# A gated cross-attention block: the four heads interleaved, the warming products and the second input moved, and a new order for the fill

## The chip, the cores and the metric

One core of a Trainium2 chip (trn2). The metric is the device time of one execution in microseconds (us). The kernel is written engine by engine: TensorE (PE: matrix products and transposes), VectorE (DVE), ScalarE (ACT), GpSimd (POOL), and SyncE (SP), which issues most DMAs. Each engine works through its own list in order; semaphores tie the lists together.

## What is computed

```python
x = x + tanh(g_xattn[0]) * xattn(layernorm(x), ctx, mask, rms_scale, q_w, kv_w, out_w)
x = x + tanh(g_ffn[0])   * ffn(layernorm(x), W1, b1, W2, b2)

def xattn(x, mem, mask, rms_scale, q_w, kv_w, out_w):        # 4 heads, 1 key/value head, 64 wide
    xn, mn = rmsnorm(x, rms_scale), rmsnorm(mem, rms_scale)
    q = rope(einsum('BTD,NDH->BTNH', xn, q_w), S + t) / 8
    k, v = einsum('BSD,cKDH->cBSKH', mn, kv_w);  k = rope(k, s)
    p = softmax(where(mask, q k^T, -2.4e38));    return einsum('BTNH,NHD->BTD', p v, out_w)

def ffn(x, W1, b1, W2, b2):                                   # weights made ternary: -1, 0 or 1
    return gelu(x @ ternary(W1).T + b1) @ ternary(W2).T + b2
```

x is 4 x 1024 x 256, the context 4 x 154 x 256, the FFN 1024 wide; all float32.

## The kernel before

The 4096 rows of x are eight groups of 512 (four tiles of 128 rows), two groups to each of the four batches. A group goes through: transposing x (`x_T`), projecting it to q (`project`, `q`), the rotation (`rotate` on DVE with `rope`, `add_rotated` on POOL), transposing q (`q_T`), the scores of two heads at a time (`scores`), mask and row minimum (`mask_and_min`), exponentials (`exps`), division (`normalise` on POOL), transposing the probabilities (`p_T`, `tail_T`), the product with values that have Wo already in them (`attend`), residual, second normalisation, and the FFN (`ffn_in`, gelu, `ffn_out`). To keep float32 accuracy in the quick fp32r format, every operand is split into a rounded part ("hi", on ACT) and a remainder ("lo", on DVE), and products are made of two or three such pairs. FFN work of a group is done in the step after its attention.

The order of the work is written out by hand for each engine: a function `fill` for what comes before the loop, which is the preparation of the weights and groups 0 (`FIRST`) and 1 (`SECOND`) woven together (`BEFORE` is the group ahead of the first), and a function `step` that runs for groups 2 to 9, the last two of which only finish. Semaphores count in that order. The lists `FILL_T`, `FILL_M` and `FILL_H` name the order in which the pairs of PSUM banks `ps_t`, `ps_m` and `ps_h` are used, and so which use waits for which.

What the fill prepares:
- `keep_warm` makes products of ones that nobody reads. `spread_pairs` and `spread_rows` put the RMS scales onto partitions, by products with a single row; `gate_row` holds the two gate values and comes by a DMA of its own.
- The context (`ctx_sb`) is transposed (`context_T`), scaled while it is copied (`copy_context`), and multiplied by Wk (`k_products`) and by Wv side by side twice (`v_products`). Its norms come from `context_sums` and `context_norms` on DVE and a power on POOL.
- `rotate_k` and `add_rotated_keys` rotate the keys, `k_T` transposes them, `kk_rounded` and `kk_rest` split them into `kk_hi` and `kk_lo`. Two heads share a score product: their queries stand in partitions 0 to 63 and 64 to 127, and the keys stand once in the upper half of the partitions and once in the lower half of a second set of columns, the rest zero (two memsets of POOL).
- Wq is scaled by ACT (`scale_wq`), its column sums are made by TensorE (`sum_wq`), DVE takes off their 256th part (`centre_wq`), and ACT and DVE split it (`wq_rounded`, `wq_rest`). This takes the layernorm's mean out of x.
- `vw_product(n)`, twelve of them, multiply values by Wo; `vw_rounded` and `vw_rest` split them. `VW_ON_POOL` could name some for POOL; it is empty. `w_low_piece` on POOL and `ternary` on DVE make the FFN weights ternary, in eight pieces.

SP's DMAs in order: the context, its four tails, x of group 0, the key tables, the q tables, Wo twice, W1, W2, x of group 1, b1. ACT's: the identity, the RMS scales, the gates, Wk, Wv, Wq.

## Time and profile before

| | |
|---|---|
| median of three runs | 308.92 us (308.06 to 309.13) |
| the profiled execution | 309.19 us; its span, first to last instruction, 307.4 us |
| TensorE busy | 295.4 us (96%), 2119 products and transposes |
| DVE busy | 243.2 us (79%) |
| ACT busy | 234.3 us (76%) |
| POOL busy | 131.1 us (43%) |
| DMA | 13.27 MB, most of what the weights and tables need in the first 20 us |

The page's slices (one digit a fortieth of the span, tenths of it busy):

```
PE   5996999989999999999999999999999999999996
DVE  2589899999987889779886899878977897567443
ACT  2596787898697967897588959796788958883581
```

Times in rows count from the span's start. A row of the timeline gives start, duration, engine, line, operation, what is written and what is read ("ps_t<-ident_sb,q_cos": the moving operand first, then the one loaded as weights) and the shape. Matmuls and DVE instructions are pipelined: the next one starts before the last one's printed end, so a rate is read from starts. A float32 product shows as two instructions, an fp32r product and a transpose as one.

### The profile page before, as it was taken

How to read it: one execution, taken by the hardware profiler on the slowest of the kernel's cores; microseconds unless marked ns; L12 is line 12 of the kernel's file. 1: busy time of each engine (PE TensorE's matmuls, PEld its weight loads, DVE VectorE, ACT ScalarE, POOL GpSimd, SP SyncE). 2: the span in 40 equal slices, each digit the busy share in tenths (PEclk: the TensorE clock that was granted, in tenths of full speed). 3: DMA queues.
4: the chain of work that ended last, by engine and by line, in shares of the span. 5: the costliest groups of instructions: out<-in, count | busy, mean ns of one | idle time of the engine just before them, and what ended most of it. 6: DMA issues, size and time to landing. Idle time of an engine off the chain costs nothing.

```text
span 307.4 us, 6780 instructions
## 1 busy us (share of the span) xinstructions
PE 295.4 (96%) x2119; PEld 274.6 (89%) x2119; DVE 243.2 (79%) x819; ACT 234.3 (76%) x601; POOL 131.1 (43%) x152
## 2 busy tenths in 40 slices
PE   5996999989999999999999999999999999999996
PEld 5975999878999899989998899989998999889886
DVE  2589899999987889779886899878977897567443
ACT  2596787898697967897588959796788958883581
POOL 8376878692246305522334414630542333511300
PEclk9999899999999999999999999999999999999999
DMA  6970000200202002100201010100210000100202
GB/s 204 286 243 2 0 3 0 71 0 2 69 3 68 2 0 70 53 17 2 68 13 55 0 54 15 51 17 0 71 52 17 2 0 11 61 3 0 70 0 68
DMA packets 12281, 13.27 MB, mean 43 GB/s; under 512 B 823, under 2 KB 11696, under 8 KB 12256
## 3 DMA queue, kind: packets, MB, share of 16 engines
q1 hardware_dynamic: 11452, 12.29, 12.6%
q10 hardware_dynamic: 708, 0.46, 0.5%
q0 software_dynamic: 96, 0.21, 0.4%
q8 instruction: 13, 0.21, 0.3%
q14 instruction: 12, 0.10, 0.1%
HBM read 8.76 MB, written 4.19 MB: 42 GB/s over the span
## 4 chain that ended last, share of the span: by engine, by line
PE 85%; DVE 7%; issue 2%; ACT 2%; DMA 1%; POOL 0%; ACTq 0%; DVEq 0%
PE ps_m L1293 22%; PE ps_h L1293 22%; PE ps_m L1526 17%; PE ps_s L1293 9%; PE ps_t L1301 4%; PE ps_t L1471 4%; PE ps_t L1447 2%; DMA gate_row<-in_gates 1%; PE ps_t L1546 1%; PE ps_m L1546 1%; DVE s_neg L1025 1%; PE ps_t L1479 1%; DVE pT_lo L938 1%; ACT hT_hi L699 1%; ACT h_all L699 1%
## 5 line engine op out<-in xcount | busy, mean ns | idle before, releaser
L487 POOL TENSOR_TENSOR prob<-prob,p_inv 128x512 f32<-128x512 f32 x32 | 34.2, 1069 | 66.8 <-DVE p_inv L1041 66.7
L1086 DVE TENSOR_TENSOR hT_lo<-h_all,hT_hi 128x512 fp32r<-128x512 f32 x64 | 42.2, 686 | 18.6 <-ACT hT_hi L699 18.6
L1293 PE MATMUL ps_h<-x1nT_hi,w_tern 128*128 128x512 f32 x128 | 54.4, 425 | 1.2 <-ACT hT_hi L699 0.9
L1526 PE MATMUL ps_m<-w_tern,hT_hi 128*128 128x256 f32 x224 | 55.2, 287 | 0.0
L1526 PE MATMUL ps_m<-w_tern,hT_lo 128*128 128x256 f32 x224 | 53.6, 279 | 0.0
L665 ACT ACTIVATE prob<-s_neg,s_min 128x154 f32<-128x154 f32 x128 | 52.4, 416 | 1.2 <-DVE s_min L1036 1.1
L699 ACT ACTIVATE h_all<-ps_h,b_sb 128x512 f32<-128x512 f32 x64 | 44.6, 697 | 8.2 <-PE ps_h L1293 7.0
L1293 PE MATMUL ps_h<-x1nT_lo,w_tern 128*128 128x512 f32 x128 | 50.6, 395 | 0.0
L463 POOL TENSOR_TENSOR q_cos<-q_cos,q_sin 128x256 f32<-128x256 f32 x32 | 23.6, 738 | 58.4 <-DVE q_sin L992 57.6
L1293 PE MATMUL ps_m<-vw_hi,pT_hi 128*128 128x256 f32 (+1 forms) x160 | 45.5, 284 | 0.0
L1293 PE MATMUL ps_m<-vw_hi,pT_lo 128*128 128x256 f32 (+1 forms) x160 | 44.8, 280 | 0.0
L1293 PE MATMUL ps_m<-vw_lo,pT_hi 128*128 128x256 f32 (+1 forms) x160 | 44.7, 279 | 0.0
L699 ACT ACTIVATE hT_hi<-ps_h,b_sb 128x512 fp32r<-128x512 f32 x64 | 44.7, 698 | 0.0
L1526 PEld LDWEIGHTS ps_m<-w_tern,hT_lo 128*128 128x128 f32 x224 | 42.2, 188 | 0.0
L1526 PEld LDWEIGHTS ps_m<-w_tern,hT_hi 128*128 128x128 f32 x224 | 42.1, 188 | 0.0
L938 DVE TENSOR_TENSOR pT_lo<-ps_t,pT_hi 128x512 fp32r<-128x512 f32 (+1 forms) x64 | 30.2, 482 | 10.8 <-ACT pT_hi L642 10.7
L642 ACT ACTIVATE pT_hi<-ps_t 128x512 fp32r<-128x512 f32 (+1 forms) x64 | 27.3, 444 | 9.0 <-PE ps_t L1471 8.8
L1293 PEld LDWEIGHTS ps_m<-vw_hi,pT_hi 128*128 128x128 f32 x160 | 30.0, 188 | 1.2
L1293 PEld LDWEIGHTS ps_h<-x1nT_hi,w_tern 128*128 128x128 f32 x128 | 24.1, 188 | 7.4 <-ACT hT_hi L699 3.8
L1293 PEld LDWEIGHTS ps_m<-vw_lo,pT_hi 128*128 128x128 f32 x160 | 30.1, 188 | 0.6
L1293 PEld LDWEIGHTS ps_m<-vw_hi,pT_lo 128*128 128x128 f32 x160 | 30.0, 187 | 0.0
L642 ACT ACTIVATE qT_hi<-ps_t 128x256 fp32r<-128x256 f32 x32 | 12.1, 377 | 23.2 <-PE ps_t L1447 23.2
(162 smaller groups left out, 778.2 us busy)
## 6 DMA issues: line engine op xcount, KB each, us to landing
x_sb<-in_x SPq DMA_DIRECT2D x8, 512.0 KB, 3.5
out_x<-x_both SPq DMA_DIRECT2D x8, 384.0 KB, 2.5
h_all<-in_w1t SPq DMA_DIRECT2D x1, 1024.0 KB, 11.1
w_raw<-in_w2t SPq DMA_DIRECT2D x1, 1024.0 KB, 13.4
out_x<-x_both SPq DMA_DIRECT2D x8, 128.0 KB, 1.7
x_both<-in_ctx_main SPq DMA_DIRECT2D x1, 512.0 KB
wo_raw<-in_wo SPq DMA_DIRECT2D x2, 256.0 KB, 8.4
x_both<-in_wq ACTq DMA_DIRECT2D x1, 256.0 KB, 6.5
```

The source lines that it names most:

```text
L463: pool.tensor_tensor(q, q, swapped, ALU.add).then_inc(q_roped, 1)
L487: pool.tensor_tensor(main, main, inv.to_broadcast([P, H, P]), ALU.mult)
L642: nc.scalar.activation(dst, src, ACT.Copy).then_inc(t_hi, 1)
L665: e = nc.scalar.activation(prob[t][:, h, :], s_neg[t % 2][:, h, :], ACT.Exp, bias=s_min[t % 2][:, h:h + 1], scale=-1.0, accum_out=p_sum[:, ...
L699: g = nc.scalar.activation(dst, ps_h[c % 2][:], ACT.Gelu, bias=b1_sb[:, c:c + 1])
L938: dve.tensor_tensor(dst, src, hi, ALU.subtract).then_inc(t_lo, 1)
L1086: dve.tensor_tensor(hT_lo[:, c, :], h_act[c % 4][:], hT_hi[:, c, :], ALU.subtract).then_inc(h_split, 1)
L1293: m = pe.matmul(dst, lhs, rhs, start=(n == 0), stop=(n == len(pairs) - 1))
L1301: m = pe.transpose(dst[:, P * t:P * (t + 1)], src[:, t, P * k:P * (k + 1)], ident_sb[:])
L1447: m = pe.transpose(t_bank(s.i, f"q{t}")[:, P * a:P * (a + 1)], q_cos[t % 2][:, P * a:P * (a + 1)], ident_sb[:])
L1471: m = pe.transpose(t_bank(s.i, f"p{t}")[:, P * h:P * (h + 1)], prob[t][:, h, 0:P], ident_sb[:])
L1526: m = pe.matmul(dst, a[:, c, P * t:P * (t + 1)], w[:, c, :], start=(c == 0 and a is hT_hi), stop=(c == NF - 1 and a is hT_lo))
```

## The change

It has five parts. `SPLIT_ON_POOL` and the waits it brings in are empty: they yield the same waits as before.

1. *Interleaved heads.* Wq's columns are ordered so that a channel's four heads stand side by side (column = channel x 4 + head). The rotation reads the projection once and writes both products with one instruction of 128x512 on DVE, with a joined table `rq`, made on POOL in the fill by two copies. POOL's addition works on halves of 128 columns. `q_T` loads every other column of q. The keys stand doubled in neighbouring columns, and a parity column (1 or 0 for each partition) scales them into `kk_hi` and `kk_lo`, over all 128 partitions, so the two memsets go.
2. *Centring by a product.* A matrix (identity minus 1/256, scaled by row) is multiplied by Wq on TensorE; ACT and DVE split the result out of PSUM. `scale_wq`, `sum_wq` and DVE's `centre_wq` go.
3. *Warming.* `keep_warm` multiplies ones by 512 columns of zeros: four times before `spread_pairs`, once after. The later six products of ones go. `k_products` takes Wk and Wv side by side (128 columns; the second half is not used).
4. *DMAs.* The RMS scales go first on ACT's queue, two of the context tails move to it, the gates go last and have a product of their own (`spread_gates`). The second input is fetched before the q tables; group 0's transposed x lies in `x1nT_hi` and `x1nT_lo`, so group 1's need not wait for its use.
5. *Another order of the fill* on TensorE, ACT, DVE and POOL, and of the banks. All twelve value remainders are on DVE, as before. The order of `step` is the same.

```diff
@@ SP: DMAs
-            for b in range(B):
+            for b in range(2):
                 sp.dma_start(ctx_sb[TP * b:TP * b + TAIL, B, :], ctx_tail[b]).then_inc(ctx_in, 16)
...
+            sp.dma_start(x_sb[1][:], x_g[1]).then_inc(x_in[1], 16)
+            sp.dma_start(rq_cos, rope_q_cos).then_inc(rope_in, 16)
+            sp.dma_start(rq_sin, rope_q_sin.rearrange("p t j c -> p t (j c)")).then_inc(rope_in, 16)
...
-            sp.dma_start(x_sb[1][:], x_g[1]).then_inc(x_in[1], 16)
@@ POOL
-            pool.memset(kk_hi[:].bitcast(F32), 0.0).then_inc(zeros_set, 1)
-            pool.memset(kk_lo[:].bitcast(F32), 0.0).then_inc(zeros_set, 1)
+            pool.memset(centre_base[:, 0::2, :], -1.0 / D).then_inc(base_edges_set, 1)
...
+            def join_tables():
+                pool.wait_ge(rope_in, 32)
+                pool.tensor_copy(rq[:, :, 0].rearrange("p t (j c) -> p t j c", j=2),
+                                 rq_cos.rearrange("p t (o c) -> p t o c", o=1).to_broadcast(
+                                     [P, 2 * NT, 2, C // 2])).then_inc(rope_set, 1)
+                pool.tensor_copy(rq[:, :, 1], rq_sin).then_inc(rope_set, 1)
...
+                cos, sin = (q[t % 2].rearrange("p (j n) -> p j n", j=2) for q in (q_cos, q_sin))
+                pool.tensor_tensor(cos, cos, sin[:, ::-1, :], ALU.add).then_inc(q_roped, 1)
...
                 context_rstd()
                 scale_tables()
+                mask_biases()
+                rstd1(BEFORE)
+                join_tables()
                 add_rotated_keys()
@@ ACT
+            act.wait_ge(ctx_zeroed, 1)
+            for b in range(2, B):
+                act.dma_start(ctx_sb[TP * b:TP * b + TAIL, B, :], ctx_tail[b]).then_inc(ctx_in, 16)
...
+                for k in range(KD):
+                    nc.scalar.activation(centre[:, k].rearrange("p (a c) -> p a c", c=P), centre_base[:, 1 - k:3 - k, :],
+                                         ACT.Copy, scale=scale1[:, KD + k:KD + k + 1]).then_inc(centre_set, 1)
...
+                for j in range(2):
+                    for dst, src in kk_parts(kk_hi, S * j):
+                        nc.scalar.activation(dst, src, ACT.Copy, scale=parity[:, j:j + 1]).then_inc(kk_hi_set, 1)
@@ DVE
+                        dve.scalar_tensor_tensor(dst, src, parity[:, j:j + 1], hi, ALU.mult,
+                                                 ALU.subtract).then_inc(kk_set, 1)
...
-                dve.scalar_tensor_tensor(q_cos[t % 2][:].rearrange("p (a c) -> p a c", a=2 * H),
-                                         q.rearrange("p (a c) -> p a c", a=2 * H), r, cos, ALU.mult, ALU.mult)
...
-                dve.scalar_tensor_tensor(q_sin[t % 2][:].rearrange("p (h c) -> p h c", h=H),
-                                         q.rearrange("p (h c) -> p h c", h=H), r, sin,
+                tables = rq[:, pos].rearrange("p a (c o) -> p a c o", o=1).to_broadcast([P, 2, C, H])
+                twice = q.rearrange("p (o c h) -> p o c h", o=1, h=H).to_broadcast([P, 2, C, H])
+                dve.scalar_tensor_tensor(q_both[t % 2][:].rearrange("p a (c h) -> p a c h", h=H), twice, r, tables,
                                          ALU.mult, ALU.mult).then_inc(m_read, 1)
@@ DVE, the fill from wq_rest on (new order, to mask_and_min(FIRST, 0))
+                gate_norms()
+                sums1(FIRST)
                 wq_rest()
+                mask_of(FIRST)
                 v_rest(0)
+                v_rest(1)
                 rope_first(BEFORE)
+                sums1_there(FIRST)
+                variances1(FIRST)
+                rope(FIRST, 1)
+                kk_rest()
+                q_lo(FIRST, 0)
+                gate_tail_norms()
+                rope(FIRST, 2)
+                rope(FIRST, 3)
+                q_lo(FIRST, 1)
+                mask_and_min(FIRST, 0)
@@ TensorE
+            def keep_warm(n):
+
+                pe.wait_ge(zeros_set, 1)
+                zeros = prob_tail[:].rearrange("p t h s -> p (t h s)")
                 for _ in range(n):
-                    pe.matmul(dst[:, 0:P], ones_sb[:], ones_sb[:], start=True, stop=True)
+                    pe.matmul(ps_h[1][:], ones_sb[:], zeros, start=True, stop=True)
...
+            def centre_wq():
+                pe.wait_ge(centre_set, KD)
+                pe.wait_ge(wq_in, 16)
+                for k in range(KD):
+                    m = products(ps_m[0][:, H * C * k:H * C * (k + 1)],
+                                 [(centre[:, j, P * k:P * (k + 1)], wq_raw[:, j].rearrange("p (a g c) -> p c g a", a=HP, g=2)) for j in range(KD)])
+                m.then_inc(wq_centred, 1)
...
-                    m = pe.transpose(t_bank(s.i, f"q{t}")[:, P * a:P * (a + 1)], q_cos[t % 2][:, P * a:P * (a + 1)],
+                    m = pe.transpose(t_bank(s.i, f"q{t}")[:, P * a:P * (a + 1)],
+                                     q_cos[t % 2].rearrange("p (n a) -> p a n", a=HP)[:, a],
                                      ident_sb[:])
@@ TensorE, the fill's head
-                keep_warm(5)
+                keep_warm(4)
                 spread_pairs()
-                spread_rows()
+                keep_warm(1)
                 context_tail_T()
                 context_T(0)
                 context_T(1)
-                keep_warm(2)
+                spread_rows()
                 x_T(BEFORE, 0)
+                x_T(BEFORE, 1)
                 k_products()
-                x_T(BEFORE, 1)
-                sum_wq()
+                spread_gates()
+                centre_wq()
                 v_products(0)
-                keep_warm(4, ps_s[1])
+                tail_norms()
+                v_products(1)
                 k_T()
                 q_first(BEFORE)
```

## Rows read from the trace of the kernel before

**Rows 1.** By stage: start:end, length, each engine's busy us (instructions), clock, DMA, GB/s
```profile
12.50:20.00 7.50, 7.50 (x51) 6.44 (x51) 5.11 (x18) 4.46 (x10) 3.55 (x3) 1.00 1.05 331
20.00:28.30 8.30, 5.53 (x40) 4.61 (x39) 8.14 (x22) 6.38 (x12) 5.31 (x9) 1.00 0.09 27
28.30:56.40 28.10, 27.73 (x198) 26.34 (x198) 26.93 (x114) 22.66 (x83) 23.59 (x26) 0.94 0.01 1
56.40:79.50 23.10, 21.89 (x147) 19.12 (x147) 21.90 (x63) 20.22 (x42) 12.24 (x10) 1.00 0.07 24
79.50:280.60 201.10, 199.97 (x1475) 187.68 (x1474) 164.58 (x561) 161.89 (x424) 74.33 (x88) 1.00 0.09 30
```

**Rows 2.** Chain of waits, first 80 us: start, us, what
```profile
1.87 3.88 DMA gate_row<-in_gates
...
29.50 1.46 PE ps_s L1293 x6
```

**Rows 3.** DVE in order of time, 19.9 to 31.4 us: start, us, what
```profile
19.97 0.48 DVE L989 SCALAR_TENSOR_TENSOR q_cos<-ps_m,r,rq_cos 128x256 f32<-128x256 f32 x1 [0.32 <-PE ps_m L1293]
...
20.77 1.75 DVE L909 TENSOR_TENSOR kk_lo<-ps_s,kk_hi 64x512 fp32r<-64x512 f32 x4
...
24.46 1.39 DVE L952 BATCH_NORM_STATS2 bn<-x_sb 128x6 f32<-128x256 f32 x4
...
26.47 0.29 DVE L891 TENSOR_TENSOR hT_hi<-ps_h,hT_hi 64x128 fp32r<-64x128 f32 x1
...
28.33 0.30 DVE L1025 CUSTOM_DVE_ANT_0 s_neg<-ps_s,mask_now 128x154 f32<-128x154 f32 x1
...
30.69 0.74 DVE L916 SCALAR_TENSOR_TENSOR vw_lo<-ps_h,gate_r,vw_hi 128x512 fp32r<-128x512 f32 x1
31.35 0.31 DVE L1025 CUSTOM_DVE_ANT_0 s_neg<-ps_s,mask_now 128x154 f32<-128x154 f32 x1
```

**Rows 4.** TensorE in order of time, first 20 us (xN: merged instructions)
```profile
1.28 2.50 PE L1307 MATMUL ps_h<-ones_sb 128*128 128x128 f32 x10 [1.28 <-POOL ones_sb L378]
...
11.73 2.92 PE L1293 MATMUL ps_h<-x1n,prob 128*128 128x64 f32 x20
...
15.80 1.88 PE L1293 MATMUL ps_m<-prob 128*128 128x512 f32 x4
...
17.52 1.05 PE L1307 MATMUL ps_s<-ones_sb 128*128 128x128 f32 x8
```

**Rows 5.** POOL and TensorE's key transposes in order of time, to 20 us
```profile
1.16 0.53 POOL L379 MEMSET prob_tail<- 128x512 f32 x1
...
9.33 1.19 POOL L389 TENSOR_TENSOR ctx_r<-ctx_me,neghalf 128x5 f32<-128x5 f32 x1 [2.48 <-DVE ctx_me L860]
...
15.79 1.55 POOL L404 TENSOR_TENSOR x1n<-s_neg 128x640 f32<-128x640 f32 x1 [3.43 <-DVE s_neg L885]
...
18.41 0.71 PE L1374 MATMUL ps_s<-ident_sb,x1n 128*128 128x128 f32 x5
```

**Rows 6.** DMA issues, first 30 us: count, KB each, us to landing
```profile
h_all<-in_w1t SPq DMA_DIRECT2D x1, 1024.0 KB, 11.1
...
rq_sin<-in_rope_q_sin SPq DMA_DIRECT2D x1, 256.0 KB, 8.6
```

**Rows 7.** DVE by form: count, busy us, mean ns; idle before
```profile
L916 DVE SCALAR_TENSOR_TENSOR vw_lo<-ps_h,gate_r,vw_hi 128x512 fp32r<-128x512 f32 x8 | 6.0, 747 | 0.9 <-ACT vw_hi L631 0.9
...
L909 DVE TENSOR_TENSOR kk_lo<-ps_s,kk_hi 64x512 fp32r<-64x512 f32 x2 | 1.4, 684 | 0.0
```

**Rows 8.** TensorE's waits before the half-clock stretch, in order of time
```profile
23.48 0.39 PE L1293 MATMUL ps_m<-wq_hi,xT_hi 128*128 128x256 f32 x1 [0.93 <-DVE q_sin L992]
...
28.46 0.74 PE L1293 MATMUL ps_h<-hT_lo,hT_hi 128*128 128x512 f32 x2 [1.31 <-DVE gate_r_tail L902]
```

**Rows 9.** Transposes at half clock: the context's, strided, and x_sb's, unstrided
```profile
8.32 1.92 PE L1330 MATMUL ps_s<-ident_sb,x_both 128*128 128x128 f32 x8
...
10.88 1.06 PE L1301 MATMUL ps_t<-ident_sb,x_sb 128*128 128x128 f32 x4
```

443 lines of the change are left out of this document (221 added, 222 removed), and 8 rows, old and new, of the table FILL_T.

## The prediction, made before the changed kernel ran

> **What bounds the kernel now.** I read the busy time by stage first [rows 1]. The 307.4 us fall into three parts. From 79.5 to 280.6 us six groups of rows pass through the loop's order, and TensorE is busy 199.97 of 201.10 us: it bounds that part, while VectorE (DVE) has 36.5 us to spare. From 280.6 us there is the tail. Before 79.5 us lies the fill: preparing weights, keys and values, and groups 0 and 1. There DVE is busy 8.14 of 8.30 us, then 26.93 of 28.10, then 21.90 of 23.10. A queue so full works through its own list, so the fill's end is set by when DVE starts its dense list and by how long that list is. TensorE is close behind (27.73 of 28.10 us from 28.3 on, 3.4 us of it at the granted half clock, 1.2 GHz, visible as a mean of 0.94).
>
> The chain of waits says the same and shows the head [rows 2]: it runs through a DMA of two gate values (3.88 us), TensorE's small products and then DVE, until TensorE takes over at 29.50 with the second scores. So what the change does is worth something where it starts DVE's list earlier, shortens it, or changes TensorE's work in the loop.
>
> **The point to follow.** Group 0's first mask-and-minimum starts on DVE at 28.33 us [rows 3]. I place that point in the new order and carry the shift to the end.
>
> **Warming and head.** Before, five products of ones (ten instructions) take 2.50 us from 1.28, 0.21 us apart, and TensorE then waits for the gates. The same instruction stands 0.11 apart in the eight at 17.52 [rows 4]: half and full clock. (The granted-clock figure reads 1.00 there too; the spacing is what tells.) The clock rises inside the key products (11.73 to 14.65): twenty take 2.92 us, where all at half would take 4.3. By then TensorE had worked without a break for some 7 us, since the gates' DMA landed at 5.75 [rows 2]. Now four products of 512 columns (eight instructions) start once prob_tail is zero, at 1.7 us. A 512-column instruction takes 0.43 us at full clock (value product, 1.88 us for four) [rows 4], so twice that, 0.86, at half. All at half clock they end at 1.7 + 6.9 = 8.6 us; with the clock up after half of it, at about 7. I take 7.8, both ends kept. Then the pair scales are spread, and DVE, whose queue has the context sums behind them, starts these at 7.8 + 0.75 = 8.55 instead of 6.64 (0.75 us after the gates' wait ended at 5.89). What waits behind: the context norms, ready when POOL (GpSimd) started its power at 9.33 [rows 5], 2.7 us after the sums (now 11.2); on POOL that power of 1.19 us (12.4), the key tables, the mask bias and group 0's power, together 3.0 us (15.4; their order is new, their sizes are not). New on POOL, ahead of the key addition, are two copies of 512 values (join_tables). No row shows one: a memset of 512 values takes 0.53, the two-input addition of 640 takes 1.55, so 1.24 for 512 [rows 5]; I take 0.8, being one-input, so 1.6 us, 17.0. The key addition's 1.55 us makes 18.6, against 17.34 before. That hid under the value and warming products, since the key transposes started at 18.41 [rows 5]; now they start at 18.8: +0.4 us. If the warming ends at 8.6, it is +1.2; the price of the two copies moves it by −0.5 to +0.9. The memsets of kk_hi and kk_lo go, but POOL had been done with all memsets before its power at 9.33: nothing.
>
> **Queues.** SP issues two context tails fewer and the second input (512 KB) before the tables; about 0.9 us earlier and, at the 331 GB/s of that stretch [rows 1], 1.6 us of transfer later for all behind. The tables for q, last landing 8.6 us after issue at 4.91, 13.5, then land near 14.5, before POOL asks at 15.4; wo and the two FFN weights land 1 to 1.5 us later (w1 18.1 before, about 19.6 now) [rows 6], while ScalarE (ACT) sums them only behind the keys, after 20.7. ACT issues two tails before wk, wv and wq, 0.5 us net later; wq, landing near 9.5, is asked for at 13.9. All hidden, with about 1 us of cover for the tables.
>
> **Wq centring.** Gone: ACT's two scalings and DVE's two corrections of all of Wq, and four column-sum instructions of TensorE. New: the centring matrix is scaled by ACT (the same sizes) and multiplied by Wq, eight instructions of 256 columns. At half the 0.43 us of a 512-column one [rows 4] that is 1.72 us. In order: k products 11.5 to 13.75 (20 at 0.112, since a wider moving side of 128 columns still fits the 0.11 of the ones products), gates, centring to 15.7, value products 1.9+0.4 to 18.1. wq_lo is ready at about 17.4: hidden behind k_T. Its moving operand steps 512 bytes from value to value, which no row shows; I bound it by nothing and by what the same instruction takes at half clock, a doubling, +1.7 us, of which 1.1 would be late for the first projection. The first rope then starts at 20.2 (before 19.97).
>
> The Trainium skill (Advanced Engine Details and Errata, SBUF Cachelines) says that a line is 16 bytes, and that reading a new line for every value costs; by that the doubled price would hold. It also says two hits on a line suffice, which would leave the transposes below untouched; no row at full clock shows either.
>
> **DVE up to the point.** From the first rope to the point passed 28.33 − 19.97 = 8.36 us, nearly without idling [rows 3]. Leaving it: statistics of group 1 (from 24.46) and one x remainder, together 2.01 us to 26.47, then a value remainder and the mask, 0.5; the early second input allows the first, and these go into DVE's idle time before 20 us or behind the point. Each rope was two instructions, 0.79 us from 19.97 to 20.77; now it is one of 512 values from PSUM, like the value remainder of 0.66 us (30.69 to 31.35): −0.13 each, four of them −0.5. Coming in: group 1's variance 0.49, and the key remainders as scaled subtractions (747 against 684 ns for 512 values [rows 7], two large and two small) +0.15. Sum: 8.36 − 2.5 − 0.5 + 0.65 = 6.0; 20.2 + 6.0 = 26.2, or 2.1 us earlier. TensorE's scores need the keys at 24.1 and take 1 us: in time. The first value product, which waited for DVE until 28.46 [rows 8], can start near 25.2.
>
> **From the point to the loop.** All twelve value remainders were already on DVE (VW_ON_POOL is empty on both sides): zero. The list gains x remainder 0.60, loses the variance 0.49 and five rope pairs' 0.65: −0.5 us. DVE idles only 2.4 us between 28.3 and 79.5, which an order could halve but not remove; I count nothing. TensorE at half clock cost 3.41 us × ½ = 1.7 us; it had stood still for 0.93 us and 1.31 us just before [rows 8]. (The mean of 0.94 over 28.10 us is 3.4 us at half.) In the new order it has less to wait for, but while DVE sets the pace only part counts: 0.5 of 0 to 1.7. Towards 79.5 the FFN's gelus on ACT follow and start when ffn_in does, which waits for x1n's remainders in DVE's list: they move with it. Sum: −2.1 −0.5 −0.5 = −3.1 us.
>
> **The loop and the tail.** The step orders are unchanged. Four ropes a step save DVE 0.5 us where it is not the bound; POOL's addition loses a dimension of its pattern and keeps its length: zero. The scores have the same 308 columns with other zero rows. One thing touches TensorE: q's transposes load q_cos with a step of two values. The context transposes before do the same; eight of them took 1.92 us, or 0.213 each, and the four unstrided x_sb ones at that clock took 0.213 as well [rows 9]. At full clock the unstrided stand 0.11 apart (five key transposes in 0.71 us [rows 5]). Bounds: zero, or 64 × 0.104 = 6.7 us if the strided load stays at 0.213. I take zero, the equality at half clock being the nearest row.
>
> **Sum.** The profiled run took 309.19 us: a span of 307.4 and 1.79 around it. 309.19 − 3.1 = 306.1. It is 0.27 above the median of the three runs, 308.92; against that the forecast is 305.8 us.
>
> **The rivals.**
> - *Deeper gain, 303.2.* The half-clock stretch vanishes wholly (another −1.2) and the new order removes the TensorE waits of 1.2 us from 56.4 to 79.5. For it: TensorE carries the chain from 29.5 to 45. Against: DVE is 96% busy there.
> - *Slow centring, 307.0.* The strided moving operand doubles its 1.73 us: −3.1 + 1.1 to 1.7, less the cover. It is the skill's rule above, as a mechanism of this kernel.
> - *Given back, 308 to 309.8.* The warming at half clock ends late (+0.8), the copies hold the keys (+0.5), and in the fill TensorE and ACT (20.22 of 23.10 us from 56.4 on) are near enough to full that DVE's shift is lost there.
> - *Slower, 312.5.* The strided weight loads of q's transposes. Each 0.104 us is paid by the bounding engine, 64 times; from 0.05 us each it undoes the gain. Against: the equal 0.213. This is the one that ends on the other side.
> - *It does not do what it says:* the wide products, of zeros, might not lift the clock; then the head runs at half clock to 12.7 as before, +0.8, inside the range.
>
> **Chances.** Forecast (304.3 to 307.3 or so) 0.53; slow centring 0.12; deeper 0.12; given back 0.12, mostly within the bound; strided loads 0.07; 0.04 for an order that blocks a queue somewhere I did not walk. Runs of this kernel differ by 0.3%, 0.9 us, which is what a measurement can tell from no change. Faster by more 0.76, same 0.12, slower 0.12. The range must leave out no more than 2 in 10: from 302.4 (below it half of the deeper cases) to 309.2 (the strided loads and the rest above).
>
> **What would show it.** The warming row of eight instructions ending between 7 and 8.6 us, later gaps of 0.11; copies of 0.5 to 1.1 us on POOL; centring spacing 0.216 or 0.43; the first mask-and-minimum near 26.2 us; rope rows of 0.75 us, 32 of them; a loop step still 33.5 us (201.1 over six); q's transposes 0.109 apart; and the start of group 2's loop step near 76.4 instead of 79.5. It is wrong if that start comes late although the point came early (then DVE was not the bound), or if the loop's length moves by more than 0.5 us.

## The result

The change made the kernel slower, by 0.9%: 311.37 us median of 5 runs (310.71 to 312.39) against 308.92 beside it, a ratio of 1.0093 (95% interval 1.0072 to 1.0115). I had forecast 305.8. The profiled execution of the changed kernel took 312.39 us, the longest of its five and 1.0 above their median; its span is 310.6 us against 307.4.

Three stretches say where the time went. I cut the span at the point (group 0's first mask-and-minimum on DVE) and at the end of the fill (start of group 1's fourth residual, the 79.5 us of the prediction):

| us | to the point | point to end of fill | end of fill to the end | span |
|---|---|---|---|---|
| before | 28.33 | 51.15 | 227.91 | 307.4 |
| forecast | 26.2 | 50.15 | 227.9 | 304.3 |
| after | 30.13 | 51.12 | 229.35 | 310.6 |

All three missed: the point by 3.9 us, the fill behind it by 1.0, the loop and the tail by 1.4.

The busy time by stage, cut as in [rows 1]:

```profile
12.50:20.00 7.50, 7.50 (x37) 5.03 (x36) 5.47 (x21) 2.92 (x8) 3.93 (x6) 1.00 1.05 273
20.00:30.10 10.10, 7.90 (x49) 6.18 (x49) 8.53 (x20) 8.87 (x15) 5.99 (x6) 1.00 0.24 77
30.10:56.40 26.30, 25.86 (x198) 24.33 (x197) 25.96 (x104) 22.53 (x81) 25.18 (x30) 1.00 0.01 2
56.40:81.30 24.90, 23.51 (x156) 20.13 (x154) 23.03 (x63) 21.25 (x44) 12.05 (x11) 1.00 0.07 23
81.30:283.60 202.30, 201.25 (x1476) 189.36 (x1475) 163.90 (x539) 163.14 (x424) 74.36 (x88) 1.00 0.09 29
```

The half-clock stretch is gone (0.94 in [rows 1], 1.00 here), as hoped; in one of the other four runs the mean clock of the whole run was 0.994, which is what one such stretch leaves. But the DMAs moved 273 GB/s between 12.5 and 20 us where they had moved 331, and were still at work behind 20 us. DVE stands idle for 1.6 of the 10.1 us before the point, where it had idled 0.2 of 8.3. And the six groups of the loop's order took 202.3 instead of 201.1 us although no instruction was added there.

TensorE, and below it ScalarE, POOL and DVE, in order of time up to the first ropes (start, us, what; in brackets the wait before it):

```profile
1.83 5.11 PE L1351 MATMUL ps_h<-prob_tail,ones_sb 128*128 128x512 f32 x8 [1.83 <-POOL prob_tail L396]
...
11.79 1.09 PE L1343 MATMUL ps_t<-ident_sb,x_sb 128*128 128x128 f32 x8 [1.48 <-DMA x_sb<-in_x]
...
15.35 3.76 PE L1335 MATMUL ps_m<-x_both,prob 128*128 128x256 f32 x8
18.94 1.90 PE L1335 MATMUL ps_m<-prob 128*128 128x512 f32 x4
...
21.60 0.66 PE L1427 MATMUL ps_s<-ident_sb,x1n 128*128 128x128 f32 x4
```

```profile
20.95 1.06 ACT L651 ACTIVATE hT_lo<-wo_raw 128x1024 fp32r<-128x1024 f32 x1 [1.20 <-DMA wo_raw<-in_wo]
21.92 0.58 ACT L639 ACTIVATE hT_hi<-ps_m 64x512 fp32r<-64x512 f32 x1
...
23.73 1.75 ACT L647 ACTIVATE kk_hi<-ps_s,parity 128x512 fp32r<-128x512 f32 x4
```

```profile
18.88 0.61 POOL L409 COPY rq<-q_both 128x512 f32<-128x512 f32 x1 [2.39 <-DMA q_both<-in_rope_q_sin]
19.44 0.60 POOL L412 COPY rq<-q_both 128x512 f32<-128x512 f32 x1
20.01 1.54 POOL L427 TENSOR_TENSOR x1n<-s_neg 128x640 f32<-128x640 f32 x1
```

```profile
23.14 0.69 DVE L933 TENSOR_TENSOR hT_hi<-ps_m,hT_hi 64x512 fp32r<-64x512 f32 x1 [1.50 <-ACT hT_hi L640]
...
24.08 0.75 DVE L1032 SCALAR_TENSOR_TENSOR q_both<-ps_m,r,rq 128x512 f32<-128x512 f32 x1
```

Three chains end within half a microsecond of each other, each late. The value products end at 21.5. TensorE had stood 1.48 us waiting for group 0's own input, which is issued ahead of the early second one and 0.8 us sooner than before, and yet landed at 11.8 instead of 10.3 us; and the eight centring products took 3.76 us, 0.45 apart. These started at 15.35, right behind the products ahead of them: wq had landed at 15.0 and was not waited for. The key addition ends at 21.55, behind two copies that waited for rq_sin until 18.88 and themselves took 0.6 each. And ScalarE waited for wo until 20.95, rounds it ahead of the values, and so gave DVE the values at 23.1; DVE forms their remainders ahead of the first rope. That rope came at 24.08, forecast 20.2. Whoever takes one chain away finds the next. The DMA issues show why they are late, against [rows 6] (last column: us from issue to landing):

```profile
h_all<-in_w1t SPq DMA_DIRECT2D x1, 1024.0 KB, 14.1
...
wo_raw<-in_wo SPq DMA_DIRECT2D x2, 256.0 KB, 10.7
x_both<-in_wq ACTq DMA_DIRECT2D x1, 256.0 KB, 11.4
q_both<-in_rope_q_sin SPq DMA_DIRECT2D x1, 256.0 KB, 14.2
```

Wo and Wq in the kernel before:

```profile
wo_raw<-in_wo SPq DMA_DIRECT2D x2, 256.0 KB, 8.4
x_both<-in_wq ACTq DMA_DIRECT2D x1, 256.0 KB, 6.5
```

### The profile page after: what moved, and what is told of

It reads as the page before. It is cut to its first block, busy times and chain, and to the rows that moved or that the text cites. A ratio compares the mean times of both kernels' runs of the same rounds, so it can differ in the third digit from the quotient of the medians.

```text
span 310.6 us, 6748 instructions
## 1 busy us (share of the span) xinstructions
PE 299.0 (96%) x2111; PEld 272.4 (88%) x2111; DVE 243.3 (78%) x787; ACT 235.6 (76%) x601; POOL 130.6 (42%) x153
## 3 DMA queue, kind: packets, MB, share of 16 engines
q1 hardware_dynamic: 11374, 12.23, 12.5%
## 4 chain that ended last, share of the span: by engine, by line
PE 76%; DVE 9%; DMA 4%; ACT 3%; issue 3%; SPq 2%; POOL 2%; DVEq 0%; ACTq 0%
PE ps_m L1335 20%; PE ps_h L1335 20%; PE ps_m L1580 17%; PE ps_s L1335 7%; DMA wo_raw<-in_wo 4%; PE ps_t L1343 4%; PE ps_t L1525 4%; PE ps_t L1500 2%; DVE s_neg L1064 1%; DVE vw_lo L958 1%; PE ps_t L1600 1%; PE ps_m L1600 1%; DVE pT_lo L980 1%; PE ps_t L1533 1%; DVE q_both L1032 1%
## 5 line engine op out<-in xcount | busy, mean ns | idle before, releaser
L1580 PE MATMUL ps_m<-w_tern,hT_hi 128*128 128x256 f32 x224 | 56.2, 289 | 0.0
L1580 PE MATMUL ps_m<-w_tern,hT_lo 128*128 128x256 f32 x224 | 54.7, 282 | 0.0
L486 POOL TENSOR_TENSOR q_both<-q_both 128x256 f32<-128x256 f32 x32 | 24.2, 760 | 58.9 <-DVE q_both L1032 58.7
L675 ACT ACTIVATE qT_hi<-ps_t 128x256 fp32r<-128x256 f32 x32 | 12.2, 382 | 23.1 <-PE ps_t L1500 22.3
## 6 DMA issues: line engine op xcount, KB each, us to landing
x_both<-in_wq ACTq DMA_DIRECT2D x1, 256.0 KB, 11.4
```

The source lines that it names most:

```text
L486: pool.tensor_tensor(cos, cos, sin[:, ::-1, :], ALU.add).then_inc(q_roped, 1)
L675: nc.scalar.activation(dst, src, ACT.Copy).then_inc(t_hi, 1)
L1580: m = pe.matmul(dst, a[:, c, P * t:P * (t + 1)], w[:, c, :], start=(c == 0 and a is hT_hi), stop=(c == NF - 1 and a is hT_lo))
```

## The experiments

The table has each run's profile cut at the same two places, the median of all its runs and the ratio to the kernel before. Landings of the first DMAs differ from execution to execution, so "to the point" of a single profile is uncertain by about 1 us (28.33, 27.27 and 27.26 in before, e7 and e14, whose engines have the same work there); the other two repeat within 0.5 us where code and tiles are the same, and the last stretch lies between 227.88 and 227.93 in all four profiles of the old layout. Differences of a few tenths are read from it, not from medians.

| run | to the point | fill behind it | to the end | median us | ratio (95%) |
|---|---|---|---|---|---|
| e1_x1_behind_tables | 31.04 | 51.13 | 229.09 | 311.26 | 1.0078 (1.0056 to 1.0101) |
| e2_wq_contiguous | 28.45 | 50.74 | 229.13 | 310.73 | 1.0078 (1.0049 to 1.0106) |
| e3_both | 29.77 | 51.11 | 228.89 | 311.52 | 1.0060 (1.0022 to 1.0098) |
| e4_fill_order | 30.61 | 51.76 | 229.30 | 311.96 | 1.0096 (1.0066 to 1.0125) |
| e5_v_before_wo | 30.16 | 51.02 | 229.22 | 311.88 | 1.0085 (1.0056 to 1.0113) |
| e6_after_padded | 29.25 | 51.19 | 228.81 | 310.52 | 1.0054 (1.0030 to 1.0077) |
| e7_before_shifted | 27.27 | 50.79 | 228.90 | 309.86 | 1.0073 (1.0025 to 1.0121) |
| e8_three | 26.80 | 51.03 | 228.73 | 309.43 | 1.0019 (0.9989 to 1.0049) |
| e9_q_halves | 28.27 | 51.00 | 228.37 | 310.40 | 1.0057 (1.0029 to 1.0084) |
| e10_keys_first | 27.48 | 51.06 | 228.77 | 309.38 | 1.0024 (1.0001 to 1.0046) |
| e11_before_x1_early | 31.67 | 51.16 | 227.91 | 310.09 | 1.0048 (1.0012 to 1.0083) |
| e12_tails_on_sp | 26.95 | 51.03 | 228.75 | 309.19 | 1.0012 (0.9991 to 1.0033) |
| e14_before_tails_on_act | 27.26 | 51.03 | 227.93 | 308.93 | 1.0020 (0.9985 to 1.0055) |
| e15_pad_992 | 28.36 | 50.99 | 228.16 | 308.91 | 1.0011 (0.9985 to 1.0037) |
| e16_before_wide | 26.91 | 49.97 | 227.88 | 307.32 | 0.9956 (0.9924 to 0.9988) |
| e17_all_x1_late | 27.24 | 52.46 | 228.17 | 311.66 | 1.0086 (1.0057 to 1.0115) |
| e18_fill_and_fixes | 27.05 | 51.43 | 228.24 | 308.81 | 1.0016 (1.0000 to 1.0033) |

**Two suspects for the head, alone and together.** e1 moves the second input behind the query tables and its sums behind the mask copy:

```diff
-            sp.dma_start(x_sb[1][:], x_g[1]).then_inc(x_in[1], 16)
             sp.dma_start(rq_cos, rope_q_cos).then_inc(rope_in, 16)
             sp.dma_start(rq_sin, rope_q_sin.rearrange("p t j c -> p t (j c)")).then_inc(rope_in, 16)
+            sp.dma_start(x_sb[1][:], x_g[1]).then_inc(x_in[1], 16)
```

> The changed kernel (311.4 us) with one part undone: the second input is loaded behind the two query tables and ahead of wo, and its sums stand behind the mask copy on DVE. Theory A (the early second input delays what the head needs: rq_sin landed at 18.88 us and held POOL's joining copies, the key addition and so k_T at 21.6): rq_sin lands 3 us earlier, near 16, the key addition ends near 18.6, and k_T is then held by the value products (20.84 in the trace of after): 0.8 us earlier, 310.6 us. If wq lands earlier too (it landed at 15.0), the value products come forward with it and 2 to 2.5 us are gained, 309.2. Theory B (the strided centring alone holds the head): k_T is set by the PE's centring and value products either way, at most 0.3 us, 311.1.

Neither theory's time came. The key addition ended at 19.74 us, 1.8 earlier, and k_T still started only at 23.29, behind the products:

```profile
13.76 3.30 PE L1335 MATMUL ps_h<-x1n,prob 128*128 128x128 f32 x20
...
17.30 3.76 PE L1335 MATMUL ps_m<-x_both,prob 128*128 128x256 f32 x8
...
23.29 0.71 PE L1427 MATMUL ps_s<-ident_sb,x1n 128*128 128x128 f32 x5
```

The profiled run, 313.05, is not typical of its median: TensorE fell to half clock there from about 12.3 to 15.7 us (the twenty key products took 3.30 us, 2.40 in after, and the transposes ahead of them 1.87 instead of 1.09). Without these 1.7 us the products would have let k_T start near 21.6, as in after. So the tables alone were not what held it: the two chains ended together.

e2 orders wq's columns on the host:

```diff
-                                 [(centre[:, j, P * k:P * (k + 1)], wq_raw[:, j].rearrange("p (a g c) -> p c g a", a=HP, g=2)) for j in range(KD)])
+                                 [(centre[:, j, P * k:P * (k + 1)], wq_raw[:, j]) for j in range(KD)])
```

> The changed kernel with the columns of wq put in interleaved order on the host, so that the centring products read a contiguous moving operand; the same is computed. The eight centring products should be 0.22 us apart and no more 0.44, and take 1.8 instead of 3.8 us. Theory B (this is what the head lost): k_T and the first rope come 1.8 us earlier, 309.6 us. Theory A (k_T waits for the key addition behind the late tables, until 21.55 whatever the PE does): k_T does not move, 311.2 us, within 0.3 of the changed kernel.

The centring row of e2's profile:

```profile
15.03 1.99 PE L1335 MATMUL ps_m<-x_both,prob 128*128 128x256 f32 x8
```

So the strided moving operand had cost 1.8 us for eight instructions. In this profile rq_sin and wo landed earlier too, and the point came 1.7 us earlier; the median moved by 0.6. e3, both edits:

> Both edits of the two runs before together. If the two waits stand beside each other (key addition at 21.55, value products at 20.84), each alone hides behind the other and only both together bring k_T forward: to 18.8 to 19.3 us, 2.3 to 2.8 us earlier, 308.8 us, more than the sum of the two alone. If only one of them held the head, this equals that one.

k_T came at 19.07 us, as the joint theory said, and yet the first rope only at 23.72: 4.65 us behind it. That pointed at the third chain. TensorE, ScalarE and DVE:

```profile
19.07 0.71 PE L1427 MATMUL ps_s<-ident_sb,x1n 128*128 128x128 f32 x5
...
20.60 1.06 ACT L651 ACTIVATE hT_lo<-wo_raw 128x1024 fp32r<-128x1024 f32 x1 [3.12 <-DMA wo_raw<-in_wo]
...
23.72 0.75 DVE L1032 SCALAR_TENSOR_TENSOR q_both<-ps_m,r,rq 128x512 f32<-128x512 f32 x1
```

The medians of e2 and e3 carry something else besides. In both profiles TensorE fell to half clock between about 24 and 28 us, after it had stood still for 1.11 and 0.91 us (e2) and for 3.04 us (e3), waiting for DVE and POOL; thirteen of their fourteen runs have a mean clock of 0.988 to 0.994, against one of five of the changed kernel. What this took back of their gain is not separated here.

**The third chain: wo.** In all five profiles until then the first rope stood 3.1 to 3.4 us behind the rounding of wo. e5 moves that rounding behind the values on ScalarE:

```diff
-                wo_rounded()
                 v_rounded(0)
                 v_rounded(1)
+                wo_rounded()
                 kk_rounded()
```

> The changed kernel with one move in ScalarE's order: wo_rounded() stands behind the two v_rounded() instead of ahead of them. Theory W: the first rope waits for wo. In all five profiles of the changed kernel and its variants the first rope starts 3.1 to 3.4 us after wo_rounded (20.95 to 24.08, 21.59 to 24.99, 18.88 to 22.00, 20.61 to 23.72, 21.44 to 24.57), whatever k_T does, because ACT rounds wo ahead of the values and DVE forms v_rest ahead of the rope. Then the first rope comes at about 22.8 (values end at 21.5 in after), 1.2 us earlier, and starts no more at wo_rounded plus 3.1; time 310.3 us against 311.4. Rival (k_T, the key addition and the value products set it): first rope stays 2.5 us behind k_T, time 311.3.

```profile
22.81 1.06 ACT L651 ACTIVATE hT_lo<-wo_raw 128x1024 fp32r<-128x1024 f32 x1
...
23.16 0.75 DVE L1032 SCALAR_TENSOR_TENSOR q_both<-ps_m,r,rq 128x512 f32<-128x512 f32 x1
```

Theory W held for the rope, which came at 23.16, 1.7 us behind k_T and 0.35 behind the start of wo's rounding. It gained nothing: ScalarE's list was as long as before, with the keys' rounding still behind wo (22.81 + 1.06). DVE waited for it and then for q's rounding, 0.28 us each, and the point stayed at 30.16. Alone, the edit only changes which wait ends last.

**The loop.** Between the two kernels the products with w2 (ffn_out) had moved from 117 to about 120 ns apart, in every profile (the mean of 342 gaps in the loop is 117.2 ns in before and 119.4 in after). Their code is the same. What differs is where the tiles lie: the new tile parity and the larger tables push hT_hi and hT_lo up by 1056 bytes per partition, 32 modulo 64. Two runs test that from both sides:

```diff
         parity = sb("parity", [P, 2])
+        pad = sb("pad", [P, 8])
```

> The changed kernel with 32 bytes per partition of unused SBUF laid behind the small tile parity, so that every tile behind it has the address it had in the kernel before modulo 64 bytes; no instruction is changed. Theory P (the loop lost to the place of the tiles: hT_hi and hT_lo moved by 32 bytes modulo 64, and the products with w2 went from 117 to 120 ns apart in each profile of the changed kernel): these products are 117 ns apart again, a loop step takes 0.15 to 0.19 us less, time 310.3 us against 311.4. Rival D (the loop lost to q_T's strided reads, 0.123 against 0.109 to 0.117 us apart): the products stay at 120 ns, the step stays, 311.4.

```diff
         gate_r_tail = sb("gate_r_tail", [P, B])
+        pad = sb("pad", [P, 8])
```

> The kernel before with 32 bytes per partition of unused SBUF laid behind gate_r_tail: every tile behind it has its address of the changed kernel modulo 64 bytes, and no instruction is changed. Theory P: products with w2 go from 117 to 120 ns, a loop step takes 0.15 to 0.19 us more, 310.0 us against 308.9. Rival D: nothing, 308.9.

The same set of sixteen products in the fourth group, first and last of them, in four kernels: before, after, before with the 32 unused bytes (e7), and e15 below.

```profile
150.57 0.37 PE L1526 MATMUL ps_m<-w_tern,hT_hi 128*128 128x256 f32 x1
...
152.42 0.28 PE L1526 MATMUL ps_m<-w_tern,hT_lo 128*128 128x256 f32 x1
```

```profile
152.79 0.36 PE L1580 MATMUL ps_m<-w_tern,hT_hi 128*128 128x256 f32 x1
...
154.67 0.28 PE L1580 MATMUL ps_m<-w_tern,hT_lo 128*128 128x256 f32 x1
```

```profile
149.37 0.36 PE L1527 MATMUL ps_m<-w_tern,hT_hi 128*128 128x256 f32 x1
...
151.24 0.28 PE L1527 MATMUL ps_m<-w_tern,hT_lo 128*128 128x256 f32 x1
```

```profile
150.61 0.36 PE L1581 MATMUL ps_m<-w_tern,hT_hi 128*128 128x256 f32 x1
...
152.44 0.28 PE L1581 MATMUL ps_m<-w_tern,hT_lo 128*128 128x256 f32 x1
```

First to last: 1.85, 1.88, 1.87 and 1.83 us. The means of the 342 gaps are 117.2, 119.4, 119.4 and 116.8 ns, and 118.4 in e6; this stretch has 448 such products, and 2.2 ns for each make 1.0 us. The unused bytes alone make the old kernel's products as slow as the new one's, and its last stretch 0.99 us longer (227.91 to 228.90; the medians, 309.86 against 308.88, are looser, with four of e7's ten runs at 312.8 or more). In the changed kernel the same 32 bytes won back about 0.4 us of it, not all (228.73 to 228.81 in four profiles, against 228.89 to 229.35 in six without them): there the tiles agree with the old layout modulo 64, but not modulo 128. Theory P stands; its size fits on the old side and comes to half on the new one.

e9 takes the other suspect away. It keeps e6's bytes:

```diff
-                                     q_cos[t % 2].rearrange("p (n a) -> p a n", a=HP)[:, a],
+                                     q_cos[t % 2][:, P * a:P * (a + 1)],
```

> The changed kernel with the 32 unused bytes of the run after_padded, and with q_T transposing the two contiguous halves of a q tile instead of its even and odd columns; the heads are mixed up by it, so this leaves the right scores out and only its time is read. Theory D (strided reads of q_T cost the loop what is left after the place of the tiles): the stretch from the end of the fill to the end of the span was 227.9 us in the kernel before, 229.4 in the changed one, 228.8 with the bytes; it falls to 228.0, with q_T's transposes back at 109 to 117 ns apart, and the time to 309.7 us. Rival (it is the rope's form on DVE and POOL, 743 and 760 ns, not the transposes): the stretch stays at 228.8 and the time at 310.5 us.

q's transposes from the end of the fill on (columns: count, busy us, mean ns of one), in before, after and e9:

```profile
L1447 PE MATMUL ps_t<-ident_sb,q_cos 128*128 128x128 f32 x48 | 9.2, 273 | 0.0
```

```profile
L1500 PE MATMUL ps_t<-ident_sb,q_both 128*128 128x128 f32 x48 | 9.7, 283 | 0.0
```

```profile
L1501 PE MATMUL ps_t<-ident_sb,q_both 128*128 128x128 f32 x48 | 9.1, 271 | 0.0
```

The last stretch fell by 0.4 us, to 228.37 from the 228.73 to 228.81 of the four profiles with e6's bytes, and the transposes went back to the old length: theory D holds for that much, 12 ns for each of the 48 by the rows and some 8 by the stretch. What the stride lengthens is the load of the weights: 198 ns in e6 and 139 in e9, most of it hidden behind the product ahead. The median (310.40 against 310.52) doesn't resolve it.

**Putting repairs together.** e8 has e2, e5 and e6:

> The changed kernel with three edits: the values rounded ahead of wo on ACT, the 32 unused bytes, and wq's columns interleaved on the host so that the centring products read contiguously (they took 1.99 instead of 3.76 us in the run with that edit alone). Theories W and P and the shorter centring together: first mask-and-min at 27.5 to 28.0 instead of 30.1, loop step back at 33.57; 311.4 - 2.3 - 1.1 = 308.0 us, level with or 0.3 per cent under the kernel before. If the landings of the DMAs hold the values too (wq landed at 15.0), only 1.2 of the 2.3 come: 309.1.

The point came at 26.80 us, and 1.9 us of the median were back. e10 adds a swap on POOL:

```diff
-                join_tables()
                 add_rotated_keys()
+                join_tables()
```

> The kernel of the run e8_three with one more move: on POOL the key addition stands ahead of the two joining copies. In that run's profile the key addition could start at 15.7 (last key product) but stood behind the copies, which waited for rq_sin until 16.2, and k_T came at 18.94, 0.7 us behind the value products. Then k_T comes right behind the value products, first rope 0.6 us earlier, and a late rq_sin costs only what it is later than about 18.6: 308.8 us against 309.4, level with the kernel before. Rival (wo's landing and the values' rounding hold the first rope as before): 309.4.

No gain (309.38). In its profile the key addition ended at 17.99, and k_T, at 18.77, stood right behind the products: the first half of the expectation. But the first rope stayed at 20.47, since the values' remainder on DVE ended just ahead of it.

**The landings.** e11 is the kernel before with the early second input alone:

```diff
             sp.dma_start(rk_sin[:], rope_k_sin).then_inc(tab_in, 16)
+            sp.dma_start(x_sb[1][:], x_g[1]).then_inc(x_in[1], 16)
```

> The kernel before with one part of the change alone: the DMA of the second input is issued right behind rk_sin, ahead of the query tables, wo, w1t and w2t; its sums stay where they were. Theory L (late landings are what the head lost): wq, rq_sin and wo land 1.6 to 5 us later than 9.3, 13.5 and 15.1 us. ScalarE rounds wo first and wq, the values and the keys behind it (wo_rounded at 15.8 in the kernel before), so all of them move with wo's landing, and the first mask-and-min moves from 28.3 to between 29.2 and 31.6: 310.4 us against 308.9. Rival (the cover of 1 us that I had counted holds): first mask-and-min within 0.4 us, 308.9 us.

It costs: 310.09 against 308.73 beside it, a ratio of 1.0048. That is the sign and the size of theory L, but the profile doesn't show its cause: wk, wv and wq landed as before (wq 6.3 us after issue), rq_sin 1.5 us later, at 15.0, and no engine waits for rq_sin or wo. (Its profiled run, 312.54, is not typical of its median: TensorE stayed at half clock there until about 20 us, so its 31.67 is no measure of the landings.)

e14 and e12 look for what held wk, wv and wq, which landed 2 to 4 us later in the changed kernel's profiles. e14 is the kernel before with the tails of batches 2 and 3 on ScalarE's queue, e12 is e10 with them back on SyncE's:

```diff
+            act.wait_ge(ctx_zeroed, 1)
+            for b in range(2, B):
+                act.dma_start(ctx_sb[TP * b:TP * b + TAIL, B, :], ctx_tail[b]).then_inc(ctx_in, 16)
```

> The kernel before with one part of the change alone: the DMAs of the context tails of batches 2 and 3 are issued by ScalarE ahead of wk, wv and wq instead of by SyncE. In every profile of the changed kernel and its variants wk, wv and wq land late (5.7 to 6.2, 7.0 to 8.7 and 7.8 to 11.4 us after issue, against 3.5 to 3.7, 4.0 to 4.9 and 5.4 to 6.5 in the three profiles of the kernel before and its variants, the early second input alone included). Theory T (the tails on ScalarE's queue, and the x_sb, tables behind them issued 0.8 us earlier on SyncE's, are what held wk, wv and wq): wv lands more than 2 us and wq 2 to 4 us later than in the kernel before, first mask-and-min 0.5 to 1.5 us later, 309.6 us. Rival (it is something else in the changed kernel, such as the masks' and b2's loads on POOL 1.9 us earlier): landings as in the kernel before, 308.8.

> The kernel of the run e10_keys_first with all four context tails issued by SyncE again, as in the kernel before. Theory T: wv and wq land 2 to 3 us earlier, the context sums no later; centring starts at about 13 instead of 14.55, first rope 1 us earlier if wo allows; 308.5 us against 309.4. Rival: the landings are those of e10_keys_first within 0.5 us, 309.4.

e14: 308.93, no difference, with wk, wv and wq 1.0, 0.6 and 0.7 us longer from issue to landing. e12: wk landed 4.0 and wv 6.1 us after issue instead of 5.7 and 7.0, the median moved by 0.2. In the changed kernel's order the tails do show in the landings: wk, wv and wq took 4.0 to 4.1, 4.2 to 6.1 and 6.0 to 7.2 us in the three profiles with all tails on SyncE (e12, e17, e18), and 5.7 to 6.2, 7.0 to 8.7 and 7.8 to 11.4 in the eleven with two on ScalarE. Why they do so there and hardly in e14 is not settled. Nor does it matter to the time: in none of these fourteen profiles does an engine wait for wq.

**The place of the tiles once more.** e15 is e10 with 992 unused bytes instead of 32, so that the tiles lie exactly 2048 bytes above their old places:

> The kernel of the run e10_keys_first with 992 instead of 32 unused bytes, so that every tile behind them lies exactly 2048 bytes above its place in the kernel before, not only at the same place modulo 64. Theory P2 (the place counts modulo more than 64: 0.46 us of the loop and the tail are left that neither the 32 bytes nor q_T explain): the stretch from the end of the fill to the end, 228.8 us, falls to 228.4, time 309.0. Rival (the rope's new form on DVE and POOL costs it): 228.8 and 309.4.

The last stretch fell further, from 228.77 to 228.16 us, and the products are at the old distance (the fourth pair of rows above). Theory P2 holds. With the 0.4 us of q's transposes this accounts for all that loop and tail lost: 229.16 (the average of the six profiles with the changed kernel's layout; after itself had 229.35), minus 1.0 for the place, minus 0.4 for the transposes, is 227.8, against 227.91. Which of the moved tiles matters was not tried.

**The wide warming alone.** e16 is the kernel before with its first warming products widened:

```diff
                 pe.wait_ge(const_set, 2)
-                keep_warm(5)
+                pe.wait_ge(zeros_set, 1)
+                for _ in range(3):
+                    pe.matmul(ps_h[1][:], ones_sb[:], prob_tail[:].rearrange("p t h s -> p (t h s)"), start=True, stop=True)
```

> The kernel before with one part of the change alone: its five small warming products (128 columns) are replaced by three of 512 columns on zeros. In the changed kernel's profiles TensorE ran at its full clock from 4.5 to 4.9 us on, in the kernel before from 12.5 to 12.7, and in one profile of it with the early input only from about 20 us, where key and value products took 9.6 instead of 5.8 us. Theory H (the wide warming gains what I forecast): full clock before 6 us, the eight context transposes at 1.1 instead of 1.9 us, first mask-and-min 0.7 us earlier, 308.0 us, and no run above 311. Rival (the input's landing at 10.3 and wo's at 15.1 hold the head): median within 0.3 of 308.7; the runs above 311 may still go.

It is the fastest version of this study: 307.32 us, 0.44% faster than the kernel before (0.9924 to 0.9988) and 1.3% faster than the change. TensorE and one row of DVE in its profile:

```profile
1.84 4.89 PE L1555 MATMUL ps_h<-prob_tail,ones_sb 128*128 128x512 f32 x6 [1.84 <-POOL prob_tail L379]
...
8.35 1.12 PE L1330 MATMUL ps_s<-ident_sb,x_both 128*128 128x128 f32 x8
...
10.61 2.42 PE L1293 MATMUL ps_h<-x1n,prob 128*128 128x64 f32 x20 [0.23 <-ACT prob L571]
```

```profile
26.91 0.31 DVE L1025 CUSTOM_DVE_ANT_0 s_neg<-ps_s,mask_now 128x154 f32<-128x154 f32 x1
```

The eight context transposes take 1.12 instead of 1.92 us [rows 9], the twenty key products 2.42 instead of 2.92 [rows 4], and the point comes 1.4 us earlier than in before's profile, though only 0.35 earlier than in e7's and e14's, which have the old warming. A second gain lies behind it: 49.97 us to the end of the fill, against 50.79 to 51.16 in the four other profiles of the old order. The row of that stretch:

```profile
26.90:53.80 26.90, 26.54 (x198) 24.89 (x198) 26.63 (x114) 22.58 (x83) 23.54 (x26) 1.00 0.01 2
```

28.10 us at a mean clock of 0.94 [rows 1] have become 26.90 at 1.00, with the same instructions. TensorE did not fall to half clock there, although it had stood still just before for 0.9 and 1.3 us as in [rows 8]. But this is not so in every run. Six of the twelve have a mean clock of 1.00 (median 306.5 us), the other six 0.993 or 0.994 (308.1), as have 33 of the 35 runs of the kernel before beside them; the profiled one, 306.57, is of the first six. So with the wide warming the later fall is rarer, by what is not shown, and the runs without it are 1.5 us faster than those with it.

**The early input in the changed kernel's own order.** e17 has all repairs (e12's and 992 bytes) and loads the second input last, its sums behind the first mask-and-minimum:

```diff
                 mask_and_min(FIRST, 0)
+                sums1(FIRST)
                 weight_scales()
+                sums1_there(FIRST)
+                variances1(FIRST)
```

> The changed kernel with everything taken out that the runs found to cost time, and its interleaved heads, wide warming and new order kept: values rounded ahead of wo, wq interleaved on the host, key addition ahead of the joining copies, all tails issued by SyncE, 992 unused bytes, and the second input loaded last again, with its sums and variances on DVE behind the first mask-and-min. If the early input costs the landings of wq, rq_sin and wo 1 to 2 us and its sums (1.4 us on DVE) are worth as much where they now stand, this is level with the run that keeps the early input: end of the fill near 77.5, 308.3 us. If the landings count for more: first mask-and-min near 26.0 and 307.5 us, level with the kernel before plus wide warming (307.3). If the sums count for more: 308.9 us.

Slower than any of the three cases: 311.66. The landings came forward by 1 us (wq at 8.7 us against 9.9 in e12, rq_sin at 13.9 against 14.9), but nothing had waited for them: centring started at 14.53, right behind the key products and the gates' product, as e12's did at 14.03. And the sums, now in DVE's full list, lengthened the way from the first to the second mask-and-minimum from 3.49 to 4.93 us. The profile explains 1.1 us of the 2.5 by which its median is above e12's; most of the rest goes with the clock: five of its eight runs have a mean of 0.993 or 0.994 and took 311.6 us or more, the other three 309.36 to 310.26, while all twelve of e12's are at 0.999 or 1.00. In this order, then, the early input is worth its place, by about 1 us at the same clock (e17's 992 unused bytes, worth 0.6 us, counted in) and by more where it keeps TensorE from half clock.

**The order in the fill.** e4 undid a piece of the new order behind 61 us:

```diff
-                x_lo(SECOND, 0)
-                sums1(SECOND)
                 x1n_lo(SECOND, 0)
                 x1n_lo(SECOND, 1)
                 vw_rest(11)
                 inverse(SECOND, 3)
+                x_lo(SECOND, 0)
+                sums1(SECOND)
```

(the transposes and roundings likewise on the other two engines).

> The changed kernel with one piece of its order undone on all three engines: the second group's normalised x1 tiles are transposed, rounded and their remainders formed before x_T(SECOND, 0), and DVE forms x_lo(SECOND, 0) and sums1(SECOND) behind the last value remainder. Theory C (the fill loses 1.8 us between 55.7 and 70 us because 1.9 us of DVE work stands ahead of x1n_lo and the FFN): first gelu 1.8 us earlier, end of the fill 1.5 us earlier than 81.25, 309.7 us. Rival (DVE carries the same work to the end of the fill in either order, or the table load and the gelus set it): the first gelu comes earlier but the end of the fill stays within 0.4 us, 311.2 us.

> The kernel of the run e12_tails_on_sp (values rounded ahead of wo, wq interleaved on the host, key addition ahead of the joining copies, tails on SyncE) with 992 unused bytes, and with the order between 61 and 68 us put back on all engines: x1's transposes, roundings and remainders ahead of x_T(SECOND, 0) and, on ScalarE, ahead of exps(SECOND, 3), and tail_T(SECOND, 2) behind the first FFN chunk, where the run e4_fill_order had left both. Theory C (the changed kernel's first gelu is late because x1n_lo starts 9.2 us after residual(FIRST, 3) against 7.3 in the kernel before): first gelu 1.3 to 1.8 us earlier, that is 38.0 to 38.4 us behind the first mask-and-min instead of 39.7, and the end of the fill with it; 308.7 - 1.5 = 307.2 us. Rival (the work only changes places, as in e4_fill_order): first gelu 39.5 to 40.4 us behind the first mask-and-min, 308.7 us or more.

Both rivals won. In e4, x1n_lo waited for ScalarE, which had the exponentials ahead of it, and then TensorE for x_lo:

```profile
64.25 1.29 DVE L980 TENSOR_TENSOR x1nT_lo<-ps_t,x1nT_hi 128x512 fp32r<-128x512 f32 x2 [0.70 <-ACT x1nT_hi L675]
...
66.84 0.69 DVE L980 TENSOR_TENSOR xT_lo<-ps_t,xT_hi 128x512 fp32r<-128x512 f32 x1 [0.82 <-ACT xT_hi L675]
```

In e18 x1n_lo did start 2.1 us earlier (32.65 us behind the point, in after 34.74), and DVE then waited 1.29 us for the last value rounding, now behind those exponentials. The first gelu stood 40.4 and 40.1 us behind the point, in after 39.8. A piece put back isn't the old order: what stood next to it had been moved too.

## Why the prediction was wrong

The sign, the size and the range were wrong; 311.37 lies 2.2 us above its upper end. Step by step:

- **What bounds the kernel** was read rightly, and so was the way from the first rope to the point: forecast 6.0 us, it took 6.05. Ropes of 0.75 us came as forecast (736 to 751 ns), the copies cost 0.61 instead of 0.8 each, and the warming row ended at 6.9 where I had 7 to 8.6 (6.9 to 8.6 over the fourteen profiles that have it). One slip: the +0.4 us on the key transposes put the first rope at 20.4, not at the 20.2 that the sum goes on with.
- **Wq centring: a term was mis-sized.** I took 0.216 us for each of eight instructions and put the doubling into a rival at 0.12. It took 0.45, 3.76 us for the row, and 1.99 with a contiguous operand (e2). The Trainium skill's rule (Advanced Engine Details and Errata, SBUF Cachelines) is that a new line for every value costs, and the trace agrees. The row that I could have weighed it by was not in the trace; a rule with a mechanism should have had more weight than an absence of rows.
- **Queues: "all hidden, with about 1 us of cover" failed.** I allotted 1.6 us of transfer to 512 KB at 331 GB/s, and that only to what stands behind it. Group 0's own input, ahead of it, took 9.6 us to land instead of 7.3, and TensorE waited 1.48 us for it. rq_sin landed 18.9 us into the span, forecast 14.5, and POOL waited 2.39; wo came near 20.9, and ScalarE waited 1.20. wq landed at 15.0, forecast 9.5, and here "hidden" held: nothing waited for it. Of wo I had written only that it lands 1 to 1.5 us later, and never asked who stands behind wo_rounded: the values, the keys, and through DVE's list the first rope. The transfer rate was no constant either, 273 against 331 GB/s in that stretch. With centring contiguous and the values ahead of wo on ScalarE (e8, e12) the point stands at 26.80 and 26.95, against the 26.2 forecast, in profiles whose landings were earlier too. So the head's reasoning held where its prices did.
- **From the point to the loop: −1.0 forecast, 0.0 measured.** The half-clock stretch did vanish, in four runs of five, and e16 shows what that is worth in the old order: 0.8 to 1.2 us, more than the 0.5 I took. The new order needed 51.1 us at full clock for what the old does in 50.0. The step that failed is that a list shorter by 0.5 us ends 0.5 us sooner. Which part of the order gives the 1.1 us back is not settled; e4 and e18 put one piece back and met new waits.
- **The loop: zero forecast, +1.4 measured.** "The step orders are unchanged" was true and not enough. The strided loads of q's transposes, my rival at 6.7 us, cost 0.4; the equality at half clock that I took them from was a fair guide. The other 1.0 us came from where tiles lie, which I had not considered at all. My own sign of being wrong came up here: the loop moved by 1.2 us, from 201.1 to 202.3.
- **The rivals.** Slow centring was right and too cheap at 307.0: it met late landings that I had ruled out. The one named "slower", 312.5, landed near the time, for a reason that gave 0.4 us of it. The deeper gain's mechanism exists, but the old order had it.

**The parts of the change, by their own runs:** wide warming −1.5 us; early second input +1.4 in the old order, and about 1 us gained in the new; strided centring 1.8 us on TensorE, hidden or not by the other chains; placement +1.0, q's strided transposes +0.4, tails on ScalarE nothing measurable. With the repairs (e15 308.91, e18 308.81) the changed kernel is level with the one before. As the wide warming alone gives 1.5 us, the interleaved heads, the centring product and the new order together cost about as much; which of them, beyond the 1.1 us of the fill, is open.

## What to carry to other kernels

When a transfer is moved ahead, list every DMA around it with its landing, those issued just before it too, and for each the queue of the engine that waits for it, with what stands behind that wait; here it was not the tile wanted first but the one rounded first. When several chains end together, undoing one shows nothing: e1 and e5 alone moved no median, while e8 moved it by 1.9 us. When runs of one kernel differ, look at their clock first: an edit can change how often TensorE falls to half clock, and one profile shows one case of it. And when an unchanged loop changes its pace, compare the addresses of its tiles before the code: a new tile of 8 bytes shifted all behind it.
